# Graph network on one core: raw fp32 edge features in 32-row TensorE tiles instead of bf16 parts, and every sixth batch picked on chip instead of every seventh

## The reference, cut to what matters

```python
# layer 1: x is the layer's input, one row for each node
norm_h = x / max(|x|, 1e-12)
p = exp(e - seg_max[src]) / seg_sum[src]            # e = beta * edge_weight
x = layernorm(x + (1 + eps) * x + segment_sum(norm_h[src] * p[:, None], dst))

# layer 2
h = concat([x[src], edge_attr_32], -1) @ W1 + b1    # (edges, 128 + 32) @ (160, 256)
h = gelu(layernorm(h) * g1 + be1)
agg = segment_sum(h @ W2 + b2, dst)
```

## Time and profile before

| | us |
|---|---|
| Runs | 5516.4, 5519.98, 5498.99 (median 5516.4) |
| Profiled execution, its own time | 5502.47 |
| Its span in the profile | 5500.7 |
| Mean granted clock of PE | 0.912 |
| First to last gather in the edge stage of layer 1 | 2567.5 to 3423.1 |
| First to last gather in the edge stage of layer 2 | 3505.7 to 4486.9 |

### The profile page before, as it was taken

One profiled execution on the slowest core, in us unless ns is written; L12 is line 12 of the kernel. 1 busy time (PEld: TensorE's weight loads), 2 busy tenths in 40 slices (PEclk: granted clock), 3 DMA queues, 4 the chain that ended last, 5 costly groups with the idle time before them and its releaser, 6 DMA issues.

```text
span 5500.7 us, 93752 instructions
## 1 busy us (share of the span) xinstructions
PE 4667.1 (85%) x27053; PEld 3382.8 (61%) x27130; DVE 4598.5 (84%) x13377; ACT 3625.0 (66%) x12258; POOL 4078.2 (74%) x3715
## 2 busy tenths in 40 slices
PE   4899999999999999976888888488888886999995
PEld 3787777777777777755555555355555554545553
DVE  5899999999999999976888888588888876777776
ACT  4777777777777777752777776267677763555552
POOL 4788888888888888874777776577777755777776
PEclk7889999998999999987999899699999998999997
DMA  8867666666666666653677676466666652555553
GB/s 234 160 159 175 158 160 154 158 163 152 154 160 157 163 149 160 160 90 97 201 200 200 196 202 187 130 209 211 211 208 211 213 163 84 162 155 158 159 160 105
DMA packets 614740, 919.53 MB, mean 167 GB/s; under 512 B 104056, under 2 KB 324338, under 8 KB 613954
## 3 DMA queue, kind: packets, MB, share of 16 engines
q1 hardware_dynamic: 394530, 565.04, 32.5%
q0 software_dynamic: 219680, 348.31, 29.6%
HBM read 616.90 MB, written 299.48 MB: 167 GB/s over the span
## 4 chain that ended last, share of the span: by engine, by line
POOL 45%; issue 20%; PE 14%; DVE 13%; DMA 5%; ACT 2%; SPq 1%; POOLq 0%; DVEq 0%; ACTq 0%
POOL arena L1726 26%; POOL tab L1370 9%; POOL arena L1388 9%; PE PS L1889 2%; DMA arena<-T,srcI 2%; PE PS L2230 2%; DMA tab<-arena 2%; POOL arena L1421 2%; PE PS L1684 1%; PE PS L2208 1%; DVE arena L1173 1%; DVE arena L1138 1%; PE PS L986 1%; PE PS L988 1%; DVE arena L1146 1%
## 5 line engine op out<-in xcount | busy, mean ns | idle before, releaser
L1726 POOL DMA_INDIRECT arena<-T,srcI x2112 | 2020.8, 957 | 779.8 <-issue 631.5
L1370 POOL DMA_INDIRECT tab<-arena x680 | 1122.1, 1650 | 222.0 <-issue 205.5
L1388 POOL DMA_INDIRECT arena<-T,srcI x784 | 797.7, 1017 | 287.2 <-issue 282.0
L1713 DVE TENSOR_TENSOR_SCAN arena<-arena,PS 128x512 f32<-128x512 bf16 x588 | 748.3, 1273 | 162.2 <-PE PS L2535 82.8
L1693 ACT ACTIVATE arena<-PS 128x512 f32<-128x512 f32 x588 | 348.2, 592 | 635.8 <-PE PS L1684 635.8
L1793 DVE TENSOR_SCALAR arena<-PS,nodeid 128x512 bf16<-128x512 f32 x908 | 627.2, 738 | 75.7 <-PE PS L1774 75.7
L2517 PE MATMUL PS<-arena 128*128 128x512 bf16 x2323 | 550.7, 384 | 4.4 <-issue 0.4
L986 PE MATMUL PS<-We,arena 65*128 65x256 f32 x1568 | 490.6, 395 | 70.4 <-DVE arena L1046 50.2
L1889 PE MATMUL PS<-arena 128*128 128x396 bf16 x2800 | 542.6, 351 | 8.7 <-DVE arena L1793 7.3
L789 PE MATMUL PS<-arena 128*128 128x448 bf16 x2184 | 527.3, 400 | 0.8 <-DVE arena L802 0.8
L988 PE MATMUL PS<-arena 128*128 128x256 f32 x1568 | 481.4, 388 | 0.0
(11 more groups left out here) (319 smaller groups left out, 10945.0 us busy)
## 6 DMA issues: line engine op xcount, KB each, us to landing
H<-arena SPq DMA_DIRECT2D x784, 256.0 KB, 2.3
arena<-keepR SPq DMA_DIRECT2D x294, 256.0 KB, 4.7
arena<-wF SPq DMA_DIRECT2D x98, 512.0 KB, 5.2
arena<-T,srcI POOLq DMA_INDIRECT x2896, 3.6
arena<-in_ea64T SPq DMA_DIRECT2D x98, 256.0 KB
arena<-sH SPq DMA_DIRECT2D x98, 256.0 KB, 4.7
arena<-dH SPq DMA_DIRECT2D x98, 256.0 KB, 5.0
arena<-S SPq DMA_DIRECT2D x98, 256.0 KB
```

The costliest lines, as they stand in the source:

```text
L1370: e.indirect_dma_start(out=tabs[k % KT], out_offset=at_rows(iA[b % 10][:, c:c + 1]), in_=X2[n % 3][:, c, :], in_offset=None, compute_op=AL ...
L1388: e.indirect_dma_start(out=Gs[b % NR][:, c, :], out_offset=None, in_=T0, in_offset=at_rows(srcI[:, CB * b + c:CB * b + c + 1])).then_inc(g ...
L1713: ins = e.tensor_tensor_scan(s[b % n][:, h, :], kR[g % 6][:, h0:h0 + CB * P], src[h], s[(b - 1) % n][:, h, CB * P - 1:CB * P] if b else in ...
L1726: e.indirect_dma_start(out=dst[:, c, :], out_offset=None, in_=T_tab, in_offset=at_rows(srcI[:, CB * b + c:CB * b + c + 1])).then_inc(gs.of ...
```

## The change

Layer 2's edge features are no longer cut. `pe_C` reads them as fp32 from where they already lie (`ea32T`, or `eTs` if the edges had to be sorted). Each of a pair's four quarters of 256 edges lies on its own 32 partitions, so each matmul contracts over 32 rows, and consecutive matmuls use different groups of 32 rows. A batch has four fp32 matmuls in place of eight bf16 ones. The weights W1 are held four times, once for each group of rows, in fp32. One load of 256 KB for each pair becomes four of 32 KB. Layer 1's edge stage loses the cutting (two ACT, two DVE and three SP instructions for each pair of batches), and M goes from 7 to 6. With M = 6 there are 32 picked and 164 gathered batches, in place of 28 and 168; a pick's 25 blocks are spread over five slots. A wait of ACT on its own earlier relu is added ahead of each square.

```diff
-        wX = sb("wX", [2 * P], BF16)
-        wY = sb("wY", [2 * P], BF16)
+        wX = sb("wX", [2 * P])
...
                 for n in mine:
                     k = self.on_act.index(n)
+                    t = len(self.on_act) * j + k
+                    if t >= 4:
+                        e.wait_ge(self.ohA.of(0), self.ohA.at(t - 4))
                     e.activation(self.d2[k % 4], self.sR[j % 2], ACT.Square, bias=minus[:, n:n + 1]
                                  ).then_inc(self.squared.of(0), 1)
...
-            pk = Picks(7, 0, [bank(2)], 12)
+            pk = Picks(6, 0, [bank(2)], 12)
...
-                        cut_load(e, i // 2)
...
-                    if 0 <= i - 8 < NBAT and i % 2 == 0:
-                        cut_store(e, (i - 8) // 2)
...
-                    if 0 <= i - 5 < NBAT and (i - 5) % 2 == 0:
-                        dve_cut_r(e, (i - 5) // 2)
-                    if 0 <= i - 7 < NBAT and (i - 7) % 2 == 0:
-                        dve_cut_3(e, (i - 7) // 2)
...
-                    if 0 <= i - 4 < NBAT and i % 2 == 0:
-                        act_cut_1(e, (i - 4) // 2)
-                    if 0 <= i - 6 < NBAT and i % 2 == 0:
-                        act_cut_2(e, (i - 6) // 2)
...
-                e.tensor_copy(cut[0], wC[:, :]).then_inc(own.sem, own.up())
...
-                e.tensor_copy(wY[64:96, :], cut[1][64:96, :])
...
+            def features(e, g):
+
+                c0 = g * GE
+                with e.If(unsorted["sp"] > 0):
...
+                with e.Else():
+                    for q in range(4):
+                        e.dma_start(eT[g % 3][32 * q:32 * q + 32, :], A["ea32T"][:, c0 + 2 * P * q:c0 + 2 * P * (q + 1)]
+                                    ).then_inc(ld_e.of(g), 16)
...
-                        e.dma_start(eT[g % 3], S32[:, g * GE:(g + 1) * GE]).then_inc(ld_e.of(g), 16)
+                        features(e, g)
...
-                for c in range(CB):
-                    o, r = psC[:, c * 2 * P:(c + 1) * 2 * P], slice(h0 + c * P, h0 + (c + 1) * P)
-                    e.matmul(o, eT[g % 3][:, r], wX[:, :], start=True, stop=False)
-                    ins = e.matmul(o, eT[g % 3][0:96, r], wY[0:96, :], start=False, stop=True)
+                for k in range(2):
+                    for q in range(2):
+                        c, rows = 2 * q + k, slice(32 * (b % 2 * 2 + q), 32 * (b % 2 * 2 + q) + 32)
+                        ins = e.matmul(psC[:, c * 2 * P:(c + 1) * 2 * P], eT[g % 3][rows, k * P:(k + 1) * P],
+                                       wX[rows, :], start=True, stop=True)
```

More of the change, by code:

```diff
@@ L1847, in rows_of @@
                 return G[turn_of[b] % NR] if b in turn_of else Gp[b // pk.M % 2]
[L1849 to L1862, removed]
             def sp(e):
@@ L1967, in dve @@
                         dve_sum(e, i - 2)
[L1969 to L1972, removed]
-                e.activation(e3[g % NC][:, 0, :], eq[g % NC], ACT.Copy).then_inc(c1.of(0), 1)
-            def act_cut_2(e, g):
-                e.wait_ge(r1.of(0), r1.at(g))
-                e.activation(e3[g % NC][:, 1, :], er[g % NC], ACT.Copy).then_inc(c2.of(0), 1)
             def act(e):
@@ L2013, in L1_nodes_L2_table @@
             big = arena.get(NBLK, 2 * P)
-            cut = [arena.get(2 * P, dt=BF16) for _ in range(3)]
             Y = arena.get(NBLK, P)
@@ L2100, in dve @@
                 center(e, W1ab[:, :], 2 * P, P, 0, n_c.of(0))
-                center(e, wC[:, :], 2 * P, P, 1)
+                center(e, wX[:, :], 2 * P, P, 1)
                 center(e, wD[:, :], 2 * P, P, 2)
-                e.tensor_copy(cut[0], wC[:, :]).then_inc(own.sem, own.up())
-                e.wait_ge(own.sem, own.n)
-                e.tensor_tensor(wC[:, :], wC[:, :], cut[0], ALU.subtract).then_inc(own.sem, own.up())
-                e.wait_ge(own.sem, own.n)
-                e.tensor_copy(cut[1], wC[:, :]).then_inc(own.sem, own.up())
-                e.wait_ge(own.sem, own.n)
-                e.tensor_tensor(cut[2], wC[:, :], cut[1], ALU.subtract).then_inc(own.sem, own.up())
-                e.wait_ge(own.sem, own.n)
-                e.tensor_copy(wX[0:96, :], cut[0][0:96, :])
-                e.tensor_copy(wX[96:128, :], cut[1][96:128, :])
-                e.tensor_copy(wY[0:32, :], cut[2][0:32, :])
-                e.tensor_copy(wY[32:64, :], cut[1][32:64, :])
-                e.tensor_copy(wY[64:96, :], cut[1][64:96, :])
                 p = Halves(e, own)
@@ L2153, in L2_edges @@
             kR = [arena.get(GE, dt=BF16) for _ in range(6)]
-            eT = [arena.get(GE, dt=BF16) for _ in range(3)]
+            eT = [arena.get(2 * P) for _ in range(3)]
             hT = [arena.get(2, CB * P) for _ in range(2)]
@@ L2166, in L2_edges @@
             ld_k = take("lk", NG, 6, 16)
-            ld_e = take("le", NG, 3, 16)
+            ld_e = take("le", NG, 3, 64)
             so = take("so", NBAT, NOB, 16)
@@ L2172, in L2_edges @@
             ld_w = take("ldw", 9, 1, 16)
+            def features(e, g):
+                c0 = g * GE
+                with e.If(unsorted["sp"] > 0):
+                    for q in range(4):
+                        e.dma_start(eT[g % 3][32 * q:32 * q + 32, :], eTs[64:96, c0 + 2 * P * q:c0 + 2 * P * (q + 1)]
+                                    ).then_inc(ld_e.of(g), 16)
+                with e.Else():
+                    for q in range(4):
+                        e.dma_start(eT[g % 3][32 * q:32 * q + 32, :], A["ea32T"][:, c0 + 2 * P * q:c0 + 2 * P * (q + 1)]
+                                    ).then_inc(ld_e.of(g), 16)
             def sp_nodes_ahead(e):
@@ L2212, in pe_C @@
             def pe_C(e, b):
[L2213 removed]
+                g = b // 2
                 if b % 2 == 0:
```

20 lines of the change are left out of this document (1 added, 19 removed).

## The result

| | before | after |
|---|---|---|
| Runs | 5516.4, 5519.98, 5498.99, 5511.31 | 5602.92, 5586.2, 5594.75, 5599.98 |
| Median | 5513.85 | 5597.36 |
| Profiled execution | 5502.47 | 5602.92 |
| Its span | 5500.7 | 5601.2 |

The ratio is 1.0161, with a 95% interval from 1.0147 to 1.0175: the changed kernel is slower by 1.6%. The medians lie 83.5 us apart and the two profiled spans 100.5, since the profiled execution after is the slowest of its four and the one before among the faster of its own. To see where the 100.5 us of span went, I take a stage's edge work to last from POOL's first gather of rows to POOL's first gather for the node stage behind it.

A forecast was written before the change was run, and what follows sets the result against it. Gathers bound both edge stages before; after, the pick's round bounds layer 1 (+63 us) and layer 2 stays hidden (+4). These 67 us made 5569, plus 14 to the median 5583, rounded to 5580; range 5505 to 5670.

The forecast's parts named there:

- rival 1: Both edge stages: the round of the pick bounds layer 1, layer 2 is hidden; 5580 us (5550 to 5600), chance 0.50.
- a hidden layer 2: Layer 2's edge stage: PE's longer slot stays behind the gathers, leaving some 4 us after the last gather.
- The bound of layer 1: Layer 1's edge stage: the pick's round of 28.3 us becomes the bound, above the gathers' 25.4 us.
- break-even: Layer 1's edge stage: the round of a pick below which the change pays, 26.2 us.
- The size of layer 1: Layer 1's edge stage: last pick 55 us later, then 8 us for four more batches; together +63 us.
- The cutting: Layer 1's edge stage: its removal takes 0.61 us off the pause between picks, and leaves POOL's gather issue unchanged.
- `pe_C` itself: Layer 2's edge stage: `pe_C` grows from 0.89 us to 1.4 us, five units of 0.21 plus 0.3 for mode changes.
- Rival 3: Layer 1 bound by the pick's round, and layer 2's 32-row matmuls run one after the other: 5666 us, chance 0.20.
- Layer 2's edge stage: PE needs 18.43 us for four batches against the gathers' 20.05, so 1.6 us are free; cost some 4 us.
- as the wait hides one batch in four, `pe_C` may grow by 0.54 us in each: Layer 2's edge stage: growth of `pe_C` by 0.5 us a batch stays just under the free 0.54.
- The tail: End of layer 2's edge stage: the twelve slots after the last gather cost some 4 us.
- The rest: Loads, stores and weight cutting: 0 us or some us if a load came late; weights at best -3 us.

The follow-up runs named there:

- `m6_b`: The kernel before with only M = 6 and the added wait of ACT, cutting and bf16 parts kept: 5573.12 us beside 5509.2.
- `light_b`: The changed kernel with a pick's one-hots dealt 4, 1, 5, 5, 5, 5 over the six slots: 5532.79 us beside 5505.91.
- `m6_only`: The kernel before with only M = 6 and ACT's added wait, in the group of runs some 11% slower: 6123.61 us, ratio 1.0007.
- `before_swap`: The kernel before with DVE's scaling put ahead of the square roots in layer 2's edge stage: 5504.73 us beside 5509.2.
- `same_rows`: The changed kernel with `pe_C`'s two matmuls on one group of 32 rows following each other, not alternating: 5613.92 us beside 5505.91.
- `swap_b`: The changed kernel with DVE's scaling put ahead of the square roots in layer 2's edge stage: 5564.95 us beside 5505.91.
- `half_c`: The changed kernel without the feature matmuls of every second chunk of 128 edges in layer 2: 5568.1 us beside 5509.2.

## Why the prediction came out as it did

The time of 5597.36 lies 17 us above the 5580 predicted, and layer 1 is as rival 1 has it: the round of the pick bounds it. Rival 1's other half, a hidden layer 2, didn't come true. That the total is only 17 us off is in part luck. The stages were to add 67 us and added 100.5, 33.5 more; and I added 14 us for the distance between the profiled execution and the median, where the median after lies 5.6 us below its profiled execution, which takes 19 back. Point by point:

**The bound of layer 1: right, shown.** The break-even was put at a round of 26.2 us. The round was to be 28.3 and is 28.34; in the row above its parts take 22.8 (23.2 predicted) and its pause 5.2 (5.1 predicted). The clock was to take 1.7 us from the first part and takes 1.8 on average (5.29 less 3.52). POOL's wait for PE, DVE's lost waits and ACT's unbroken work in the pause are all in the profile. `m6_b` shows that M = 6 alone does it (+62.4), and `light_b` that the chain in the pause is what makes the round: with fewer one-hots in that slot the stage falls by 87 us, to 848.1.

**The size of layer 1: 63 predicted, 59.6 measured.** From the first gather to the last matmul of the last pick it was to take 911.5 us and took 913.0 (2572.89 to 3485.9). The end behind it was to take 27.2 and took 22.4.

**The cutting: the pause right, the rest wrong.** The pause of 5.75 us had a cutting in it, and taking its 0.61 us off gave the pause after. It doesn't follow that the cutting would cost 0.6 us a round at M = 6, as I expected of `m6_only` and `m6_b`: there it stands behind the copy-out and costs 0.06. With M = 7 its removal was worth 12.4 us of stage, but through shorter gathers and not through the pause; at M = 6, where the gathers are not the bound, 2.8 (935.4 against 938.2). The prediction had said that less traffic in layer 1 can't speed up POOL, and put it at 0.

**`pe_C` itself: 1.4 us taken, 1.07 measured; the growth of a slot 0.5, measured 0.37.** Of these, 0.18 are `pe_C`, 0.10 each the longer transposes ahead of it (0.97 to the next start against 0.87 in `before_swap`) and `pe_W` (1.98 against 1.88). Rival 3, one matmul after the other with 2 us, is ruled out by the row. The prediction took five steps of 0.21 us and 0.3 for the change of mode, since "a matmul's own two passes use the same rows and can't overlap". The trace has four steps of 0.216 and 0.2 for the rest. The Trainium skill's rule on different row groups (TensorE: Matmul & The Clock Gate, Part 3: Packing small matmuls), from which I had 1.4 us, has matmuls on different groups start some 4 ns apart; the trace agrees in so far as the passes begin in pairs, most of them 7 ns apart. That the order of `same_rows` costs nothing doesn't follow from it if PE takes the matmuls strictly in the program's order. I did not try one group of rows alone, fewer columns or 64 rows.

**Layer 2's edge stage: the term that was mis-sized, 4 us predicted, 33.6 measured.** The step read: "as the wait hides one batch in four, `pe_C` may grow by 0.54 us in each". The growth was 0.37, and by that bound it was hidden. What the bound left out is that the wait itself costs more than its length once PE's clock falls behind it. Four batches without a fall took 18.43 us of PE before, and with three times 0.37 more would take 19.5, which is what the 11 rounds without low clock take. In the kernel after, the four from 3995.45 end at 4015.62, 20.17 us, with `pe_C` already at the lower clock; the four behind them take until 4037.67, 22.05 us, against the gathers' 20.05. The extra 64 us at low clock (134 against 70) cost PE about half of that in work, 32 us, an estimate from the two levels; the stage lost 33.6. In the row of `pe_W` alone the fall costs 1.8 us (3.78 against 1.98), more than the whole 1.6 us that I counted as free. Three experiments shut the alternatives out: no wait (`swap_b`) gives 1014.5 with the same matmuls, fewer matmuls with the wait (`half_c`) give 1015.8, and the order of the matmuls is worth nothing (`same_rows`). Why the low clock lasts longer than before, at a wait of the same length, is not settled. It takes both the wait and the 32-row matmuls: without the one (`swap_b`, 68 us) or the other (`m6_b`, 63 us) it is as before (70 us), and with both it stays long even when the slot has its old length (`half_c`, 114 us).

**The tail.** I took "the twelve slots after the last gather" at about 4 us. The stage's loss was nearly all there (31.5 of 33.6), since a lag of up to 14 batches is stored in the buffers and shows only once the gathers stop. Whoever reads the waits of POOL in the middle of the stage (4.6 us in 3520 to 4480) finds nothing wrong.

**The rest: right but for the gathers.** The four small loads and the nine instructions on the weights moved nothing that can be seen: the node stage took 1.6 us more, not less. That the cutting's removal would leave the gathers as they are was wrong, as said above.

## What to carry to other kernels

When work is spread over the slots of an in-order engine, ask which other engine's instruction stands behind it in the slot at the edge of the pattern: moving three one-hots, one of them of ACT with 1.2 us, from that slot to others was worth 87 us of 935, while taking the cutting away was worth 3. Judge by where an instruction stands, and not by how much work leaves the engine. A margin worked out at one clock is no margin where TensorE waits inside it; count the next instructions at twice their time and see whether it still holds. And a producer with many buffers hides a slower consumer until the end of the stage, so look at the time behind the last transfer, not at the producer's waits.

## What was not expected of the hardware

- Eight fp32 passes with a contraction over 32 rows (256 columns), on two groups of rows, take 1.07 us: they begin in four pairs, 0.216 us apart, and as much if two matmuls in a row use the same group. Four passes take 0.63 us, in two pairs. A 128-row pass of 512 columns takes 0.43.
- After a pause of 5.2 us with PE busy for 2.20 of the 5.00 us from 3003.3 on, the granted clock was 0.70 in the next 4 us (full speed and the 1.2 GHz level mixed). After a pause of 3.7 us, with PE busy for 2.18 of 3.90, it was 1.00. A cut of 1.5 us in the pause gave back another 1.2 to 2.5 us in the matmuls behind it.
- In layer 2's edge stage a wait of 1.8 us, once in four slots, goes with 134 us at low clock where 32-row fp32 matmuls stand between the full ones, and with 63 to 70 us where bf16 ones do; without the wait it is 68 and 76 us.
- Layer 1's 672 gathers took 651.9 us beside the cutting and 641.8 without it.
- In one group of runs every kernel took 11% longer, with waits on DVE, ACT and POOL that the profile puts down to no engine of the core, and in it the price of the same edit was another: M = 6 cost nothing there (1.0007) and 64 us elsewhere.
